# First layer: maxima of the later group ahead of the scores in each TensorE step

## The reference, cut to what matters

```python
q = einsum('oc,bct->bot', Wq, x) + bq      # k, v likewise, from ctx
attn = softmax(where(kv_mask, (q * scale) @ k, -inf), axis=-1)
mean = attn @ v
ex2  = attn @ (v * v)
std  = sqrt(relu(ex2 - mean * mean))
out  = (masked_instance_norm(x) * std + mean) * mask
```

## Time and profile before

| | us |
|---|---|
| median of 3 runs | 4405.9 |
| lowest and highest run | 4405.7, 4408.11 |
| profiled execution, its own span | 4404.7 |
| TensorE matmul busy | 4165.1 (95%) |
| VectorE busy | 2982.4 (68%) |
| ScalarE busy | 1964.2 (45%) |
| GpSimd busy | 1591.1 (36%) |
| maxima reductions L695 (x256), busy | 311.4, mean 1.221 |
| exponentials L582 (x256), busy | 261.1, mean 1.023 |
| weighted sums L431 (x1024 records), busy | 278.9, mean 0.623 |

### The profile page before, as it was taken

How to read it: one execution, slowest core, us unless ns; L and a number is a source line. 1 busy time by engine, 2 the same in 40 slices (tenths; PEclk the granted TensorE clock), 3 DMA queues, 4 the chain that set the end, 5 groups by cost and what they waited for, 6 DMA issues and landing times. The chain is left out here.

```text
span 4404.7 us, 70578 instructions
## 1 busy us (share of the span) xinstructions
PE 4165.1 (95%) x22060; PEld 3143.8 (71%) x22060; DVE 2982.4 (68%) x6501; ACT 1964.2 (45%) x3814; POOL 1591.1 (36%) x1094
## 2 busy tenths in 40 slices
PE   7999999778999997799999999999999999999999
PEld 3444444356777775588887797887887877988866
DVE  5666666268888887475775775767766757757743
ACT  2555555322333331355553455553555543555522
POOL 1223233145566563133234323234332234332230
PEclk7999999889999999899999999999999999999999
DMA  1000000300000000222112322222222122231122
GB/s 40 26 20 30 20 20 11 125 5 11 15 15 15 16 10 15 90 63 83 58 60 74 103 63 73 64 72 72 92 65 71 58 70 99 63 96 56 54 78 98
DMA packets 128413, 239.26 MB, mean 54 GB/s; under 512 B 16933, under 2 KB 40101, under 8 KB 126897
## 3 DMA queue, kind: packets, MB, share of 16 engines
q1 hardware_dynamic: 126544, 232.46, 16.5%
q0 software_dynamic: 1008, 3.67, 0.2%
q10 hardware_dynamic: 624, 0.18, 0.0%
HBM read 220.27 MB, written 15.73 MB: 54 GB/s over the span
## 5 line engine op out<-in xcount | busy, mean ns | idle before, releaser
L2105 POOL TENSOR_TENSOR c_wl<-c_wr,c_wh 128x512 fp32r<-128x512 f32 (+1 forms) x576 | 822.0, 1439 | 1646.0 <-ACT c_wh L2472 1388.7
L2573 ACT ACTIVATE c_pr<-c_ps,c_nms 128x257 f32<-128x257 f32 x512 | 244.2, 477 | 485.1 <-DVE c_nms L2795 483.1
L582 ACT ACTIVATE a_ex<-a_ps 128x1024 f32<-128x1024 f32 x256 | 261.1, 1023 | 259.7 <-PE a_ps L417 259.7
L1629 DVE TENSOR_TENSOR_SCAN b_sb<-b_wt,b_s,b_ps 128x256 f32<-128x256 f32 x512 | 361.6, 735 | 15.6 <-PE b_ps L1082 3.2
L695 DVE TENSOR_REDUCE a_nm<-a_ps 128x2 f32<-128x1024 f32 x256 | 311.4, 1221 | 80.5 <-PE a_ps L394 80.3
L2472 ACT ACTIVATE c_wh<-c_wr 128x512 fp32r<-128x512 f32 (+1 forms) x464 | 315.3, 687 | 45.4 <-PE c_ps L2192 41.6
L1580 POOL TENSOR_TENSOR b_sb<-b_sb,b_rt 128x1024 f32<-128x1024 f32 x128 | 277.9, 2178 | 156.5 <-DVE b_sb L1629 113.9
L2190 PE MATMUL c_ps<-c_hh,c_wh 128*128 128x512 f32 x768 | 309.1, 402 | 12.9 <-DVE c_hl L2679 12.6
L2190 PE MATMUL c_ps<-c_gh,c_wh 128*128 128x512 f32 x768 | 307.7, 401 | 5.6 <-DVE c_gl L2857 2.9
L2192 PE MATMUL c_ps<-c_hh,c_wl 128*128 128x512 f32 x768 | 304.4, 396 | 0.0
L2191 PE MATMUL c_ps<-c_hl,c_wh 128*128 128x512 f32 x768 | 303.8, 396 | 0.0
(11 more groups left out here) (379 smaller groups left out, 10578.6 us busy)
## 6 DMA issues: line engine op xcount, KB each, us to landing
c_wr<-in_downs SPq DMA_DIRECT2D x192, 256.0 KB, 2.7
c_wr<-in_wv SPq DMA_DIRECT2D x64, 512.0 KB, 3.9
c_wr<-in_wk SPq DMA_DIRECT2D x128, 256.0 KB, 2.9
c_wr<-in_wq SPq DMA_DIRECT2D x128, 256.0 KB, 2.6
c_wr<-in_fc SPq DMA_DIRECT2D x64, 256.0 KB, 2.8
b_w<-in_w SPq DMA_DIRECT2D x8, 1024.0 KB, 14.7
a_x<-in_x SPq DMA_DIRECT2D x8, 512.0 KB, 3.9
a_ctx<-in_ctx SPq DMA_DIRECT2D x8, 512.0 KB, 4.4
```

The source lines that it names most:

```text
L582: act.activation(EX[:, n % 4, :, :], ps[:, BT + 2 * (n % 2):BT + 2 * (n % 2) + 2, :], ACT.Exp).then_inc(ex_ready, 1)
L1629: mm = dve.tensor_tensor_scan(SB[:, quad % RING, pr % 2, e, 1:L + 1], WT[:, third(b, i), e, :], half(spread_bank(pair), e), S0[:, b % 2, 2 ...
L2105: pool.tensor_tensor(piece(WL, slot), piece(WR, slot), piece(WH, slot), ALU.subtract).then_inc(piece_cut[slot], 1)
L2573: act.activation(PR[:, i, 0:L + 1], ps[:, BS + 1 - i % 2, 0:L + 1], ACT.Exp, bias=NMS[:, i:i + 1], scale=float(K2) ** -0.5, accum_out=RS[: ...
```

## The change

On TensorE, in each step of a group, the pair of maxima matmuls (with its waits) is issued before the three pairs of scores matmuls (with theirs) instead of after them. The programs of all other engines stay as they are.

```diff
--- before.py
+++ after.py
@@ -447,9 +447,9 @@
 
                 it = b * G0 + g
                 for n in range(NT):
-                    scores(b, g, n)
                     if left > 1:
                         maxima(*after(b, g, 2), n)
+                    scores(b, g, n)
                     if n > 0:
                         weighted(b, g, n - 1)
                     elif not first:
```

## The result

| | before | changed |
|---|---|---|
| median, us | 4406.14 (4 runs) | 4440.67 (4 runs) |
| lowest to highest | 4405.7 to 4408.11 | 4438.96 to 4448.17 |
| ratio | | 1.0080, 95% interval 1.0066 to 1.0094 |
| profiled execution | span 4404.7 | 4448.17, span 4446.5 |
| exponentials waiting for scores, us in the profile | 259.7 | 313.9 |

34.5 us slower, where 16.5 were forecast, and 10.7 us above the range. The direction and the waits were right, the size was not.

The account below looks back on a forecast made before the run. TensorE was taken to bound the kernel; waits of 9.45 + 4.5 + 1.9 + 0.7 = 16.5 us on the median of 4405.9 gave 4422.4 us, range 4410 to 4430.

Parts of the forecast that it names:

- What bounds the layer: First layer: TensorE busy 116.33 of 117.6 us at clock 1.00, so its lost time is kernel time unless already idle.
- Scores 0.23 later, at no cost outside group 0: Every regular step: exponentials start 0.23 us later, 0.9 us remains before the weighted sum, no cost except where ScalarE bounds.
- Step 5 and the keys, 0.63 each: Step 6's leading maxima wait for the reduction delayed by the keys' low part: 15 x 0.63 = 9.45 us.
- Group 0, 0.71 each in batches 1 to 6: Group 1 starts 0.71 us late behind the mask row and last reduction; with 0.23 for batch 7, 4.5 us.
- Start of group 3, 0.27 each: Steps 0 and 1: reductions delayed by x's moments and spread hold TensorE 0.20 and 0.07 us; 7 x 0.27 = 1.9 us.
- Start of group 2, 0.1: Masking of x keeps the reduction late, so step 1 waits 0.1 us; 7 x 0.1 = 0.7 us.
- Seams at nothing: Joins between weighted sum, maxima and scores in each step cost 0, bounded by 0.10 us a step either way.
- the clock falls: Rival: some twenty new 0.6 us pauses take TensorE to 1.2 GHz, some 45 us more, 4467 us; chance 0.05.

Follow-up runs that it names:

- 2: Kernel before, with maxima leading only in step 6 of groups 1 and 2: 4438.37 us, ratio 1.0063.
- 4: Changed kernel, with scores leading again in group 0 steps 5 to 7 and group 1 steps 0 to 2: 4432.16 us, ratio 1.0054.
- experiment 3: Kernel before, with maxima leading only in group 0 steps 5 to 7 and group 1 step 0: 4442.84 us, ratio 1.0078.
- 11: Changed kernel measured again without any edit: 4439.15 us, ratio 1.0070.
- 5: Changed kernel, with VectorE cutting the keys' low part behind step 5's reduction and both mask rows behind step 5: 4460.32 us, ratio 1.0108.
- 12: Kernel before, with the first pair of scores matmuls issued three times more in step 6 of groups 1 and 2: 4419.22 us, ratio 1.0030.
- 8: Changed kernel, in group 0 ScalarE's roots moved from behind step 5 to behind step 3, keys' low part cut behind the reduction: 4415.27 us, ratio 1.0013.
- experiment 1: Kernel before, with maxima leading only in the 20 of 32 steps where the previous reduction is early enough: 4411.14 us, ratio 1.0018.
- 9: Kernel before, in group 0 ScalarE's roots moved behind step 3 and keys' low part cut behind the reduction: 4401.74 us, ratio 0.9993.
- 10: Changed kernel, group 0's roots moved behind step 3, mask rows together, keys' low part behind the reduction in groups 0 to 2: 4402.95 us, ratio 0.9992.

## Why the prediction was wrong

*What bounds the layer*: right. TensorE's lost time came out at the end, all but 1.8 us of it in this layer.

*Scores 0.23 later, at no cost outside group 0*: right; the exponentials grow no wait elsewhere.

*Step 5 and the keys, 0.63 each*: right, 0.62, and borne out by the batches of 2 and 4.

*Group 0, 0.71 each in batches 1 to 6*: right within what can be read. The mechanism, the pause of step 7 swallowing the wait of step 6 and the mask row delaying the last reduction, is in the rows above; experiment 3 has 0.8 a batch. The mask row, 0.28 us by itself, took 1.44 and ended 0.14 us behind GpSimd's operation; the Trainium skill (SBUF — State Buffer, "two separate sides") has the blocking, and the trace agrees with that.

*Start of group 3, 0.27 each*: mis-sized, 0.43. I had put 0.07 between the moments and the reduction, without a row that shows it; it was 0.22. *Start of group 2, 0.1*: 0.07.

*Seams at nothing*: right, 0.12 us in 20 steps.

In all the waits were 18.6 us against 16.5: the steps of the sum were right but for the one size, and by themselves they would have put the time at 4425, in the range.

*The step that failed is the rival "the clock falls"*, held at 0.05 with the words that pauses of 1.13 us stand in the steady loop today and the clock keeps 1.00. That was a reading of one execution: a pause that passes harmlessly seven times was taken as proof that the clock bears it, and bears it together with anything else. The runs do not bear this out. In seven profiles with falls, 20 falls in the layer behind 100 us, every one starts 3.3 to 5.9 us behind the start of the values' root in group 0, between the last 0.1 us of that same pause and 2.4 us behind its end; none stands at the new waits within groups 1, 2 and 3. In nine of them (the changed kernel, 3 and 11) the new wait of 0.42 us at the start of group 1 lies between pause and fall; the other eleven (2, 4, 5, 12) have no such wait there. Taking the pause away takes the falls away with the new waits of groups 1 to 3 in place (8 against 4), and leaving it while taking nearly all of the waits away does not (5). What the change did was to alter the timing around a pause that was already there. One reserve: the pause was taken away by moving the roots, so their place and the pause were changed together. The Trainium skill (TensorE: Matmul & The Clock Gate, "A second HAM failure mode") was nearer to it than my reading of the row: it has short idle spells that bring the clock down again and again, and the changed kernel's three stretches at 0.50 agree.

The price was off as well, on the other side: I had one step of double length behind each of 21 pauses, 45 us. In the two profiles of the changed kernel it is 3 and 2 falls, each 14 to 17 us at 0.50, and each 6.0 to 7.7 us, 21.4 and 15 us in all.

Open: why the old pause passes in some batches and not in others. The kernel before shows a fall seldom or never (in 84 executions beside the sets, two took over 4420 us, without a profile). All seven profiles with falls have batches of 96.6 us and more and the pause; experiment 1, with 95.9, has executions that are slow enough for falls, and most of experiment 12's, with 97.2, are not. Added waits bring more falls than added work of the same length. Why some falls in the last batch last 48 and 65 us is open too.

## What to carry to other kernels

When two operations of one engine can be swapped, put the one whose release comes from an engine with side work behind the one that is always ready, not ahead of it; before such a swap, look for the steps in which the releasing engine does something else first, and count them, which gave this loss to 2 us. A pause of TensorE of about a microsecond that costs only itself in one profile is no proof that it will after a change: a change of the timing around it can turn it into 6 to 9 us of low clock each time, so take it away first and judge the order afterwards. In this kernel the two orders were 1.2 us apart by their medians once the pause was gone (9 and 10), 0.4 us a batch by their profiles.

## What the hardware showed that was not expected

The granted clock fell from 1.00 to 0.50 at a pause of 0.74 to 1.4 us, in a layer in which TensorE was busy 97 us of 100, stayed there for 14 to 20 us of full work in 18 of 20 falls and for 48 and 65 us in two in the last batch, and rose again; the same pause of 1.13 us passed seven times in the kernel before. Removing waits for reductions (5) made the kernel slower, 4460.3 us for 4440.7, since the clock fell five times in its profile, once for 48 us. And VectorE stood idle for 0.22 us between the moments and the reduction behind them, a place with a drain, where I had allowed 0.07.
